# Four chained graph layers on one core: the preparation in two parts, the second one worked inside the first six items of the node stage

## The reference: what is computed

```python
def reference(x, src, dst, edge_attr_128, edge_attr_20, edge_weight, ...):
    x = _layernorm(x + _L0_gnn_ref(x, edge_index, edge_attr_128, bn_weight, ..., W1, b1, ln_weight, ln_bias, W2, b2))
    x = _layernorm(x + _L1_gnn_ref(x, edge_index, w1, b1, w2, b2, gamma, beta))
    x = _layernorm(x + _L2_gnn_ref(x, edge_attr_20, edge_weight, src, dst, W_in2f, ..., W_o2, b_o2))
    x = _layernorm(x + _L3_gnn_ref(x, edge_index, W1l, b1l, W1r, W2l, b2l, W2r))
    return x
# layer 0: hn = relu(batchnorm(x)); agg = softmax-weighted sum over 12500 edges of relu(hn[src] + edge_attr)
#          y = relu(layernorm((agg + hn) @ W1 + b1)) @ W2 + b2; returns x + y
```

## Time and profile before

| | before |
|---|---|
| median of 3 runs | 2582.02 us (2577.95 to 2592.12) |
| profiled execution, first to last instruction | span 2583.3 us |
| PE busy | 2195.1 us (85%) |
| DVE busy | 1965.6 us (76%) |
| ACT busy | 1777.9 us (69%) |
| POOL busy | 1640.3 us (63%) |

### The profile page before, as it was taken

How to read it: one execution, slowest core, us unless ns; L and a number is a source line. 1 busy time by engine, 2 the same in 40 slices (tenths; PEclk the granted TensorE clock), 3 DMA queues, 4 the chain that set the end, 5 groups by cost and what they waited for, 6 DMA issues and landing times. The chain is left out here.

```text
span 2583.3 us, 46833 instructions
## 1 busy us (share of the span) xinstructions
PE 2195.1 (85%) x14558; PEld 1832.7 (71%) x14558; DVE 1965.6 (76%) x2833; ACT 1777.9 (69%) x3703; POOL 1640.3 (63%) x1214
## 2 busy tenths in 40 slices
PE   4999999999998899999896898988788888487464
PEld 4889888998887677776664777777566666376454
DVE  5888888998896566668775899977588888487454
ACT  4788887888786577776664777766588888465221
POOL 5877756676730533427885556688557776588787
PEclk9999999999999999998888999999899999788776
DMA  3555554555555888878886677778647777576653
GB/s 102 134 151 139 129 141 136 152 147 137 139 159 162 227 258 252 251 209 216 206 218 167 137 168 173 165 206 215 180 135 203 198 199 202 125 159 163 170 158 100
DMA packets 336934, 444.74 MB, mean 172 GB/s; under 512 B 120943, under 2 KB 177093, under 8 KB 336690
## 3 DMA queue, kind: packets, MB, share of 16 engines
q1 hardware_dynamic: 216386, 377.83, 51.9%
q0 software_dynamic: 120000, 63.45, 14.0%
q10 hardware_dynamic: 304, 0.49, 0.1%
HBM read 251.01 MB, written 191.28 MB: 171 GB/s over the span
## 5 line engine op out<-in xcount | busy, mean ns | idle before, releaser
L1711 POOL DMA_INDIRECT acc<-combined,first_ x100 | 212.0, 2120 | 123.0 <-DMA acc<-combined,first_ 85.5
L452 PE MATMUL banks<-mats,g_hT 128*125 128x256 f32 x1000 | 259.5, 382 | 0.0
L472 PE MATMUL banks<-mats,g_zT 128*125 128x128 f32 x2000 | 239.2, 273 | 0.2
L472 PEld LDWEIGHTS banks<-mats,g_zT 128*125 128x125 f32 x2000 | 228.4, 188 | 0.5 <-issue 0.3
L746 POOL DMA_INDIRECT gin_xs<-x,from_ x100 | 125.2, 1252 | 162.0 <-DMA x_of_src<-gin_xs 138.0
L589 DVE TENSOR_REDUCE g_ss<-g_sq 125x4 f32<-125x1024 f32 x125 | 151.5, 1212 | 90.5 <-ACT g_sq L516 64.9
L516 ACT ACTIVATE g_sq<-banks 125x512 f32<-125x512 f32 x250 | 145.2, 593 | 101.8 <-PE banks L452 72.2
L452 PEld LDWEIGHTS banks<-mats,g_hT 128*125 128x125 f32 x1000 | 189.6, 190 | 27.1 <-issue 0.4
L381 POOL DMA_INDIRECT g_xd<-in_x,idx x100 | 129.2, 1292 | 116.8 <-PE banks L487 90.1
L533 ACT ACTIVATE g_zT<-banks,cols 128x500 f32<-128x500 f32 x250 | 179.0, 775 | 13.6 <-PE banks L460 7.9
L1771 POOL DMA_INDIRECT combined<-acc,idx x100 | 142.4, 1424 | 58.2 <-PE banks L1882 28.3
(11 more groups left out here) (390 smaller groups left out, 7068.4 us busy)
## 6 DMA issues: line engine op xcount, KB each, us to landing
x<-g_x SPq DMA_DIRECT2D x125, 224.0 KB
g_x<-in_xT SPq DMA_DIRECT2D x100, 250.0 KB
acc<-g_zero SPq DMA_DIRECT2D x101, 224.0 KB
gin_x<-x SPq DMA_DIRECT2D x50, 448.0 KB
h<-gin_hr SPq DMA_DIRECT2D x50, 448.0 KB
al_h<-h SPq DMA_DIRECT2D x40, 448.0 KB
al_x<-x SPq DMA_DIRECT2D x40, 448.0 KB
out<-al_out SPq DMA_DIRECT2D x40, 448.0 KB
```

The lines of the kernel that those rows point to most:

```text
L452: m = nc.tensor.matmul(bank[0:P, 256 * j:256 * j + 256], HT[q % 2][:, c:c + P], K.W1c, start=False, stop=j == 1)
L472: m = nc.tensor.matmul(pO[q % 2][0:P, D * j:D * j + D], ZT[q % 2][:, h, P * j:P * j + P], K.W2[:, h, :], start=False, stop=j == R - 1 and ...
L1711: pool.indirect_dma_start(out=K.acc, out_offset=bass.IndirectOffsetOnAxis(ap=K.first[:, g, r:r + 1], axis=0), in_=CR[:, g, r * D:r * D + D ...
```

## The change

`setup` keeps what the node stage reads: DVE first centres and splits the bias rows of b1 and b2 (384 columns in place of 640), builds `K.bias`, gives `split` and builds `twice`; then it centres W1 and W2, then come the batch norm columns and the index map as before. ACT widens only `bias_y` and `bias_o`, and loads 384 columns of `brows`. The rest is put in a new class, `Deferred`, whose six pieces DVE works in the node stage at the head of the turns 0 to 5 of its walk; one more DMA on SP loads the other 256 columns of bias rows. `bias_s` and `bias_u` are now written by DVE, with a broadcast over four copies, and not by ACT.

```diff
-    K.bias, K.bias_y, K.bias_o = keep("bias", [128, 640], BF16), ...
+    K.bias, K.bias_y, K.bias_o = keep("bias", [128, 384], BF16), ...
@@ setup, ACT
-                act.dma_start(rows_[:, :], I["brows"]).then_inc(rows_in, 16)
+                act.dma_start(rows_[:, :], I["brows"][:, 0:384]).then_inc(rows_in, 16)
...
-                for h in range(4):
-                    nc.scalar.activation(K.bias_s[:, 128 * h:128 * h + 128], K.bias[:, 384:512], ACT.Copy).then_inc(wide, 1)
-                    nc.scalar.activation(K.bias_u[:, 128 * h:128 * h + 128], K.bias[:, 512:640], ACT.Copy).then_inc(wide, 1)
-                act.wait_ge(wide, 14)
+                act.wait_ge(wide, 6)
@@ setup, DVE (in front of the centring of W1 and W2)
+                dve.wait_ge(rows_in, 16)
+                for a, b in ((0, 256), (256, 384)):
+                    link(nc.vector.reduce_sum(mean[:, 0:1], rows_[:, a:b], AX.X))
+                    link(nc.vector.tensor_scalar(mean[:, 1:2], mean[:, 0:1], 1.0 / (b - a), None, ALU.mult))
+                    link(nc.vector.tensor_scalar(rows_[:, a:b], rows_[:, a:b], mean[:, 1:2], None, ALU.subtract))
...
+                nc.vector.memset(mean[:, 0:1], 0.0).then_inc(split, 1)
+                dve.wait_ge(split, 1)
+                link(nc.vector.tensor_scalar(K.twice[:, :], K.ident[:, :], 2.0, -2.0 / 128, ALU.mult, ALU.add))
                 dve.wait_ge(mats_in, 16)
@@ setup, DVE (behind it)
-                dve.wait_ge(f1_in, 32)
-                for w, name in enumerate(("o2", "W2lT", "W2rT", "bo2_rows")):
...
-                for a, b in ((0, 256), (256, 384), (384, 512), (512, 640)):
...
-                link(nc.vector.tensor_scalar(K.cm[:, :], K.ident[:, :], 1.0, -1.0 / 128, ALU.mult, ALU.add))
@@ new
+class Deferred:
...
+    def load(self, sp):
+        sp.dma_start(self.rows[:, :], self.K.I["brows"][:, 384:640]).then_inc(self.rows_in, 16)
...
+    def centre(self, dve, block):
+        nc, mean = self.nc, self.mean
+        self.link(dve, nc.vector.reduce_sum(mean[:, 0:1], block, AX.X))
+        self.link(dve, nc.vector.tensor_scalar(mean[:, 1:2], mean[:, 0:1], 1.0 / 128, None, ALU.mult))
+        self.link(dve, nc.vector.tensor_scalar(block, block, mean[:, 1:2], None, ALU.subtract))
+
+    def on_vector(self, dve, n):
+        nc, K, rows, rest, part = self.nc, self.K, self.rows, self.rest, self.part
+        if n == 0:
+            self.centre(dve, K.W("o2"))
+            self.centre(dve, K.W("W2lT"))
+        elif n == 1:
+            self.centre(dve, K.W("W2rT"))
+            self.centre(dve, K.bo2_rows)
+        elif n == 2:
+            dve.wait_ge(self.rows_in, 16)
+            self.centre(dve, rows[:, 0:D])
+            self.centre(dve, rows[:, D:2 * D])
+            self.link(dve, nc.vector.tensor_scalar(K.cm[:, :], K.ident[:, :], 1.0, -1.0 / 128, ALU.mult, ALU.add))
+        elif n == 3:
+            self.link(dve, nc.vector.tensor_copy(part[0][:, :], rows[:, :]))
+            self.link(dve, nc.vector.tensor_tensor(rest[:, :], rows[:, :], part[0][:, :], ALU.subtract))
...
+        elif n in (4, 5):
+            wide = (K.bias_s if n == 4 else K.bias_u)[:, :].rearrange("p (r d) -> p r d", r=R)
...
+            self.link(dve, nc.vector.tensor_scalar(wide, part[0], K.ident[:, 0:1], None, ALU.mult))
+            for i in (1, 2):
+                self.link(dve, nc.vector.scalar_tensor_tensor(out=wide, in0=part[i], scalar=K.ident[:, i:i + 1], in1=wide,
+                                                              op0=ALU.mult, op1=ALU.add))
@@ gen_all, SP
                 load(0, 0)
                 load(1, 1)
+                df.load(sp)
                 sp.wait_ge(noded, 1)
@@ gen_all, DVE
-                walk(seq, [(-5, "edge", maximum), (1, "all", reduce), ...
+                walk(seq, [(0, "all", lambda q: df.on_vector(dve, q)), (-5, "edge", maximum), (1, "all", reduce), ...
```

More of the change, by code:

```diff
@@ L142, in setup @@
     K.wf1 = keep("wf1", [RBF, 128])
[L143 removed]
+    K.bias, K.bias_y, K.bias_o = keep("bias", [128, 384], BF16), keep("bias_y", [128, 512], BF16), keep("bias_o", [128, 512], BF16)
     K.bias_s, K.bias_u = keep("bias_s", [128, 512], BF16), keep("bias_u", [128, 512], BF16)
@@ L156, in tmp @@
             return ctx.enter_context(nc.sbuf_tensor(name, shape, dt))
-        rows_ = tmp("brows", [128, 640])
-        part = [tmp(f"bpart{i}", [128, 640], BF16) for i in range(3)]
-        rest = [tmp(f"brest{i}", [128, 640]) for i in range(2)]
+        rows_ = tmp("brows", [128, 384])
+        part = [tmp(f"bpart{i}", [128, 384], BF16) for i in range(3)]
+        rest = [tmp(f"brest{i}", [128, 384]) for i in range(2)]
         mean, mean2 = tmp("mean_w", [128, 2]), tmp("mean_w2", [128, 4])
@@ L251, in _ @@
                 nc.vector.memset(mean[:, 0:1], 0.0).then_inc(split, 1)
+                dve.wait_ge(split, 1)
+                link(nc.vector.tensor_scalar(K.twice[:, :], K.ident[:, :], 2.0, -2.0 / 128, ALU.mult, ALU.add))
+                dve.wait_ge(mats_in, 16)
+                link(nc.vector.reduce_sum(mean[:, 0:1], K.W1c, AX.X))
+                link(nc.vector.tensor_scalar(mean[:, 1:2], mean[:, 0:1], 1.0 / 256, None, ALU.mult))
+                link(nc.vector.tensor_scalar(K.W1c, K.W1c, mean[:, 1:2], None, ALU.subtract))
+                link(nc.vector.reduce_sum(mean2[:, 0:2], K.W2, AX.X))
+                link(nc.vector.tensor_scalar(mean2[:, 2:4], mean2[:, 0:2], 1.0 / 128, None, ALU.mult))
+                for h in range(2):
+                    link(nc.vector.tensor_scalar(K.W2[:, h, :], K.W2[:, h, :], mean2[:, 2 + h:3 + h], None, ALU.subtract))
                 dve.wait_ge(sq, 2)
@@ L319, in walk, with __init__, link @@
                     stage(q, seq[q][1])
+class Deferred:
+    def __init__(self, nc, K, ctx):
+        self.nc, self.K, self.count = nc, K, 0
+        self.made, self.rows_in = K.sem("df_made"), K.sem("df_rows")
+        self.rows, self.rest = [ctx.enter_context(nc.sbuf_tensor(f"df_{n}", [128, 2 * D], F32)) for n in ("rows", "rest")]
+        self.part = [ctx.enter_context(nc.sbuf_tensor(f"df_part{i}", [128, 2 * D], BF16)) for i in range(3)]
+        self.mean = ctx.enter_context(nc.sbuf_tensor("df_mean", [128, 2], F32))
+    def load(self, sp):
+        sp.dma_start(self.rows[:, :], self.K.I["brows"][:, 384:640]).then_inc(self.rows_in, 16)
+    def link(self, dve, ins):
+        self.count += 1
+        ins.then_inc(self.made, 1)
+        dve.wait_ge(self.made, self.count)
+    def centre(self, dve, block):
[19 more added lines that the diff above has]
+            self.link(dve, nc.vector.tensor_tensor(rest[:, :], rows[:, :], part[0][:, :], ALU.subtract))
+            self.link(dve, nc.vector.tensor_copy(part[1][:, :], rest[:, :]))
+            self.link(dve, nc.vector.tensor_tensor(rows[:, :], rest[:, :], part[1][:, :], ALU.subtract))
+            self.link(dve, nc.vector.tensor_copy(part[2][:, :], rows[:, :]))
+        elif n in (4, 5):
+            wide = (K.bias_s if n == 4 else K.bias_u)[:, :].rearrange("p (r d) -> p r d", r=R)
+            part = [p[:, D * (n - 4):D * (n - 3)].rearrange("p (o d) -> p o d", o=1).to_broadcast([128, R, D]) for p in part]
+            self.link(dve, nc.vector.tensor_scalar(wide, part[0], K.ident[:, 0:1], None, ALU.mult))
+            for i in (1, 2):
+                self.link(dve, nc.vector.scalar_tensor_tensor(out=wide, in0=part[i], scalar=K.ident[:, i:i + 1], in1=wide,
+                                                              op0=ALU.mult, op1=ALU.add))
@@ L686, in _ @@
                 nc.vector.memset(K.same[:, E:E + 1], 0.0)
-                walk(seq, [(-5, "edge", maximum), (1, "all", reduce), (-4, "edge", fall), (4, "all", reduce_o), (-1, "edge", share),
+                walk(seq, [(0, "all", lambda q: df.on_vector(dve, q)), (-5, "edge", maximum), (1, "all", reduce), (-4, "edge", fall), (4, "all", reduce_o), (-1, "edge", share),
                            (-2, "edge", weighted), (1, "all", lambda q: scale(q, 0)), (1, "all", lambda q: scale(q, 1)), (-7, "edge", message),
```

15 lines of the change are left out of this document (1 added, 14 removed).

## The result

The changed kernel takes 2571.64 us in the median of 20 runs (2558.13 to 2584.16), the kernel before 2584.18 in 20 (2572.51 to 2594.35). The ratio is 0.9954 with a 95% interval of 0.9938 to 0.9969: by it 11.9 us less, between 8 and 16; the two medians lie 12.5 us apart. The forecast was 8.8 us less. The measured median lies 1.6 us under the forecast time and inside the range, but the forecast time was counted from 2582.0, the median of three runs, and 20 runs put the kernel before 2.2 us higher. The change itself is 3 to 4 us larger than forecast. The bound of 0.5% lies inside the interval.

The account below looks back on a forecast made before the run. The first 60 us were taken as bound by the preparation's DVE chain and ACT's copies, then the pipe filling, then PE. Start 9.8 us sooner, less 1.0 for exposed pieces, gives 8.8 us less: 2573.2 us, range 2564 to 2584.

Parts of the forecast that it names:

- The bound of 0.5%: Whole kernel: 12.9 us, about what a measurement can tell from no change; faster by more was given 0.11 plus 0.08.
- Rival 2: Later stages: one is held by something not starting with the barrier, leaving a gain of 0 to 4 us; chance 0.10.
- Part 1: Preparation: what is left of it ends at 14.9 us, so the node stage starts 9.8 us sooner, ends 11.0 and 8.3.
- The chain behind the landing: Preparation on DVE: from the landing of the bias rows to the index map, 10.2 us.
- the landing of the rows: Preparation: the 192 KB load of bias rows lands at 4.7 us, ends 3.5 and 6.2.
- Part 2: Node stage's first turns: the six pieces on DVE cost 1.0 us in full, from pieces 2 and 3.
- Pieces 0 and 1: In front of DVE's first reduce: four centrings, 3.34 us, hidden in 7.82 us of idle time.
- Piece 2: Turn 2, before item 1's reduce: two centrings and `cm`, 1.93 us against 1.42 idle, 0.5 late.
- Piece 3: First turns of the node stage: three casts and two tensor_tensor, 1.9 us against 1.42 idle, 0.5 late.
- Piece 5: Before item 4's reduce: 2.0 us against 1.55 idle, up to 0.45 late behind a busy PE, taken at nothing.
- Collisions: Node stage's first turns: pieces' single-source instructions meet POOL's indirect DMAs, up to 0.38 us each, 0 to 3.0, taken at nothing.
- rival 1: First turns: every single-source instruction of a piece waits out a POOL DMA, 1.2 us each; 5.9 us slower, 2588; chance 0.06.

Follow-up runs that it names:

- the second comparison: The changed kernel timed once more against the kernel before, on another chip: 2536.35 against 2540.65 us, ratio 0.9979 (0.9958 to 0.9999).
- the run with the order alone: Kernel before with everything kept in the preparation, only VectorE's order changed (bias rows first, then W1 and W2): 2517.01 against 2523.44 us, ratio 0.9976.
- The second trace of the changed kernel: The unchanged program of the changed kernel, traced again on another chip: first load at 14.71 us, span 2541.6 us.
- the third: The changed kernel traced again on the chip of its second timing: first load at 14.82 us; timed there at 2536.35 us, ratio 0.9979.
- the run with 20 us added: Changed kernel with the last instruction of the preparation's chain worked 68 times more: 2536.68 against 2523.44 us for the kernel before, ratio 1.0053.
- the packed kernel: Changed kernel with index map and `twice` also out of the preparation and pieces rearranged, all matrix centrings in turn 0: 2531.48 us, ratio to before 0.9959.
- the first four runs: Order changed alone, start 20 us later, pieces at turns 40 to 45, GpSimd held until pieces 0 to 3 are through; kernel before there 2523.44 us.
- both packed kernels: The packed kernel, 2531.48 us, ratio to before 0.9959, and the same with W1 and W2 centred on ScalarE, 2530.95 us, ratio 0.9951.
- the matrices first: Changed kernel with the centring of W1 and W2 in front of the bias rows again: first load at 16.24 us, one execution 2533.70 us.

## Why the prediction was right, point by point

**Where the time was.** That the preparation is a chain whose every microsecond goes to the span was right: 20.15 us added at its end came out as 19 to 25 in the times, and in the traces of that chip what was won or lost by item 5 was there to 0.1 us at the second stage. Rival 2, the start given back, has no room left as a mechanism, though the interval of the second comparison (0.3 to 10.7) alone would allow its size. "DVE (172 of 200) has some room" was true but read too kindly: the pieces at turns 40 to 45 took 12.9 us and 9.3 of them were lost. Nothing of the forecast hung on it.

**Part 1.** The chain behind the landing was forecast as 10.2 us and took 10.25. ACT's `split` was to come 6.0 us behind the landing and came 5.9 behind; ACT was to end 2.8 ahead of DVE and ended 2.7 ahead; the handover was to be 0.9 and was 0.96. The one mis-sized term is the landing of the rows, taken at 4.7 and measured at 3.57, practically the lower end of 3.5. The middle between an unloaded tile and W1 and W2 was the wrong choice. From its issue at 0.81 this load of 192 KB took 2.8 us; the run with the order alone, with all 320 KB, took 3.5; the tile of 250 KB with nothing beside it took 3.0. The three go by size, so the load issued first wasn't held by the others behind it. With it the start moved by 10.8 us and not by 9.8.

**Part 2.** Pieces 0 and 1 hidden: right, and 1.7 us more of the same cost nothing. Piece 2: forecast 0.5 late, measured 10.92 - 9.77 = 1.15. Piece 3: forecast 0.5, measured 9.77 - 9.21 = 0.56. Item 3 then came 0.43 closer again (lead 9.64), which the sum didn't have; that TensorE's work queued up by then took up part of the lateness is a guess. Piece 5 cost 0.2 of its 0.45. At item 5 the lead was 9.36 where the sum had 8.8. The second trace of the changed kernel lost only 0.13 us from item 0 to item 5 (27.45 against 27.32), the first trace 1.56, the third 1.58 and the run with 20 us added 1.68. The forecast of 1.0 lies between, but under three of the four. "No idle of PE in the 35 us behind that" was nearly true: busy in 34.49 of the 35 us from 38 to 73 in the first trace, 34.97 and 35.00 in the others.

**Collisions.** Taken at nothing, kept at 3.0. Five of the single-source instructions of the pieces were held in the first trace, by 0.27 to 0.46 us, three of them in the exposed pieces 2 and 3: 1.2 us there. In the second trace the exposed pieces paid nothing, in the third 0.9 us. So the term should have been about 1 and not 0, and the most that one costs is 0.46 and not 0.38. All five end 0.03 to 0.11 us behind the end of POOL's DMA, and with POOL kept away all were gone. That much agrees with the lock of which the Trainium skill tells ("SBUF — State Buffer", § Who interferes with whom). What keeps it from being rival 1 is its length: instructions that start 0.13 to 0.31 us into POOL's DMA run through, the five that were held had started 0.52 to 0.68 us into it. None waited out a whole DMA of 1.2 us. The "for the whole instruction" of the Trainium skill isn't what these rows show.

**The other side.** Rival 1 would have needed 0.83 us for each of sixteen instructions; in the first trace four of the sixteen in pieces 0 to 3 paid, 0.27 to 0.46 each. It did not happen.

**The end.** The second stage began 12.8 us sooner and not 8.8; at the end 10.7 were left in the trace and 12.5 in the medians. The 3.4 us gained between item 5 and the second stage, and the 2.1 lost behind it, are of the size by which untouched stages differ between two executions, and on the quiet chip nothing was gained there. So what the change does is read at item 5: a lead of 9.36 us in the first pair of traces and 9.16 in the second, of which some 9 are expected at the end. In the first pair the start was 1.0 better than forecast and the first turns 0.6 worse; that the two misses partly cancel is luck. The 11.9 and the 5.3 of the two comparisons are this lead and the spread of everything behind it. It was right that a measurement can hardly tell this change from 0.5%.

## What to carry to other kernels

Preparation that only a later stage reads belongs in the idle time of the engine's first turns of the stage in between, in front of the first result that it waits for: there 6.6 us of VectorE (14.51 to 21.15 in the packed kernel) cost nothing, while the same kind of work in the steady state cost 70% of itself (9.3 of 12.9 us), even with another engine at 100%. In the ramp each turn's idle time is a budget: fill it and stop. And of what the first stage does need, work first on what lands first.

## What the hardware showed

- A cast or tensor_scalar (of 100 columns or more) on VectorE beside GpSimd's indirect DMAs (1.2 us each) either ran its normal time or was held until that DMA's end, and where it started decides. Read in the first 60 us of all fourteen traces and at the late pieces (250 to 300 us), beside DMAs of 1.19 to 1.24 us: all 41 that started 0.06 to 0.49 us behind the DMA's begin took their normal time; all 37 that started 0.52 to 0.86 us behind it were held, by 0.46 us down to 0.11, and ended 0.02 to 0.12 us behind the DMA; all 12 that started 1.02 us or more behind it were not held. Beside longer DMAs the bound lies elsewhere: the first DMA of the stage takes 1.40 us, and instructions 0.66 us into it ran through; so did the L629 of the earlier trace rows, 0.56 into one of 1.31. The centrings' reduces did not change (0.28 to 0.29 us). Two executions of one program differ because their instructions fall a few tenths sooner or later.
- TensorE's granted clock can fall back in a ramp: after item 0 it pauses until VectorE has scaled. In the runs with GpSimd held and with 20 us added, in both packed kernels and in the last trace of the changed kernel that pause was 1.90 to 2.23 us and the next 3.6 to 4 us were granted 0.53 to 0.60; in eight other traces it was 1.36 to 1.69 and the clock stayed at 1.00. With the order alone it was 2.15 and the clock stayed too, and behind the next pause, 2.44 in the first trace of the changed kernel and 2.48 with the matrices first, it stayed at 1.00 as well. So the length of the pause doesn't settle it, and what does stays open. Where it fell, item 2's reduce came late: 5.94 (GpSimd held) and 5.55 us (last trace) behind item 1's, against 4.97 in the second trace of the changed kernel, with the same work on VectorE.
- A DMA of 192 KB issued first landed 2.8 us after its issue (0.81 to 3.57) with 1.1 MB of others right behind it, and 320 KB in the same place 3.5 us after. The 256 KB issued second, at 1.26, took 4.5 to 4.9 us behind 320 KB and 3.8 behind 192 KB.
- Kernels that differ only in the preparation and the first turns kept step to 0.2 us from item 8 to item 124 (700 us) on the chip of the first four runs, and on the others executions of nearly the same program drifted apart by up to 7 us. Where they keep step, a trace weighs an edit of 1 or 2 us that no time here could.
